# Cross attention and mixture of experts: query weights turned first, and the places of the attention's steps in the expert loop changed

## The reference

```python
x = x + xattn(layernorm(x), ctx, ctx, mask, Wq, bq, Wk, bk, Wv, bv)   # 154 keys per batch
x = x + ffn(layernorm(x), gate_w, w_gate, w_up, w_down, sw_gate, sw_up, sw_down)

# ffn: 16 experts of width 128, the best 8 by a normed gate, and one shared expert
logits = l2norm(xf) @ l2norm(gate_w).T
scores = sigmoid(logits); topk_scores, idx = top_k(scores, 8)      # weights: topk / their sum
y = einsum('neh,ehd->ned', silu(xf @ w_gate) * (xf @ w_up), w_down)
out = sum over experts of y * weight + silu(xf @ sw_gate) * (xf @ sw_up) @ sw_down
```

## Time and profile before

| | us |
|---|---|
| median of 3 runs | 645.16 (644.83 to 646.23) |
| the profiled execution | 644.59 |
| its span | 642.5 |

### The profile page before, as it was taken

How to read it: one execution, slowest core, us unless ns; L and a number is a source line. 1 busy time by engine, 2 the same in 40 slices (tenths; PEclk the granted TensorE clock), 3 DMA queues, 4 the chain that set the end, 5 groups by cost and what they waited for, 6 DMA issues and landing times.

```text
span 642.5 us, 10415 instructions
## 1 busy us (share of the span) xinstructions
PE 632.0 (98%) x3690; PEld 550.4 (86%) x3690; DVE 462.6 (72%) x925; ACT 235.8 (37%) x500; POOL 274.5 (43%) x261
## 2 busy tenths in 40 slices
PE   7999989999999999999999999999999999999997
PEld 7688878888888888889888888898888888888886
DVE  3788797758876688767877688775896668575444
ACT  5745444323243423333242333434234332423221
POOL 2517476343632346233553336433553334423442
PEclk9999999999999999999999999999999999999999
DMA  7456653523325314233334232253240431243100
GB/s 205 100 183 187 183 149 65 198 72 102 67 35 197 108 67 98 73 129 107 93 71 166 70 137 66 34 199 97 76 99 29 171 108 41 59 121 112 65 2 33
DMA packets 112513, 67.04 MB, mean 104 GB/s; under 512 B 80982, under 2 KB 102255, under 8 KB 112463
## 3 DMA queue, kind: packets, MB, share of 16 engines
q1 hardware_dynamic: 111374, 65.61, 35.6%
q10 hardware_dynamic: 1088, 0.79, 0.4%
HBM read 55.66 MB, written 10.42 MB: 103 GB/s over the span
## 4 chain that ended last, share of the span: by engine, by line
PE 88%; DVE 3%; DMA 2%; issue 2%; POOL 2%; ACT 1%; SPq 1%; POOLq 0%; ACTq 0%; DVEq 0%
PE y_ps L397 9%; PE gate_ps L399 9%; PE up_ps L399 9%; PE y_ps L398 9%; PE gate_ps L398 9%; PE up_ps L398 9%; PE y_ps L399 9%; PE up_ps L397 9%; PE gate_ps L397 9%; PE f_ps L545 2%; POOL hidden L1358 1%; DMA cb<-c_rows 1%; PE f_ps L582 1%; DVE hs L1168 1%; PE f_ps L584 1%
## 5 line engine op out<-in xcount | busy, mean ns | idle before, releaser
L1358 POOL TENSOR_TENSOR hidden<-hidden,cb 128x512 f32<-128x512 f32 x128 | 193.0, 1509 | 281.3 <-DVE hidden L1162 237.7
L880 ACT ACTIVATE hidden<-gate_ps 128x512 f32<-128x512 f32 x136 | 81.3, 598 | 282.5 <-PE gate_ps L399 282.4
L1158 DVE SCALAR_TENSOR_TENSOR hidden<-hidden,gate_ps 128x512 f32<-128x512 f32 x136 | 92.7, 682 | 98.4 <-ACT hidden L880 98.3
L397 PE MATMUL y_ps<-W,hs 128*128 128x256 f32 x544 | 154.3, 284 | 2.3 <-DVE hs L1168 2.3
L398 PE MATMUL y_ps<-W,hs 128*128 128x256 f32 x544 | 151.5, 278 | 0.0
L399 PE MATMUL y_ps<-W,hs 128*128 128x256 f32 x544 | 151.2, 278 | 0.0
L1168 DVE TENSOR_TENSOR hs<-hidden,hs 128x512 fp32r<-128x512 f32 x136 | 102.3, 752 | 25.5 <-ACT hs L887 25.0
L397 PEld LDWEIGHTS y_ps<-W,hs 128*128 128x128 f32 x544 | 102.2, 188 | 9.4 <-issue 3.6
L397 PE MATMUL gate_ps<-xT,W 128*128 128x512 f32 x272 | 107.3, 394 | 0.0
L399 PE MATMUL gate_ps<-xT,W 128*128 128x512 f32 x272 | 107.1, 394 | 0.0
L399 PE MATMUL up_ps<-xT,W 128*128 128x512 f32 x272 | 106.9, 393 | 0.0
(11 more groups left out here) (164 smaller groups left out, 641.9 us busy)
## 6 DMA issues: line engine op xcount, KB each, us to landing
cb<-c_rows SPq DMA_DIRECT2D x64, 512.0 KB, 4.7
blocks<-in_x_dram SPq DMA_DIRECT2D x28, 128.0 KB, 2.9
xin<-in_x_dram SPq DMA_DIRECT2D x7, 512.0 KB, 4.0
t_rows<-blocks SPq DMA_DIRECT2D x28, 128.0 KB, 2.7
xs<-t_rows SPq DMA_DIRECT2D x7, 512.0 KB, 3.5
out_dram<-x SPq DMA_DIRECT2D x7, 512.0 KB, 5.6
p_rows<-blocks SPq DMA_DIRECT2D x28, 80.0 KB, 2.3
stage<-in_L_ffn_w_gate_dram SPq DMA_DIRECT2D x16, 128.0 KB, 2.6
```

The lines of the kernel that those rows point to most:

```text
L397: mm(ps, lh, rh, start=first and i == 0, stop=False)
L880: af(ew[:, i, :], gate_ps[:, i, :], ACT.Tanh, scale=0.5).then_inc(tanh_done, 1)
L1158: V_.scalar_tensor_tensor(out=ew[:, i, :], in0=ew[:, i, :], scalar=1.0, in1=gate_ps[:, i, :], op0=ALU.add, op1=ALU.mult).then_inc(silu_don ...
L1358: pg.tensor_tensor(h[:, i, :], ew[:, i, :], cb[:, pair % PLACES, (e - 1) % 2, :], ALU.mult) \
```

## The change

In the loop the tables move by half a step: `swap_p` from the end to the middle of step 2, `probs_hi` and `probs_lo` from 5 to 4.5, `attend` from (5.5, 6) to (5, 5.5), `residual`, `ln2`, `ln2_scale` and `swap_x2` by half a step likewise, and `ln2_std` from (7.5, 7.5) to (6.5, 7.5). In the first loop's DMA order `store_probs(1)` and `load_probs(1)` move ahead of one `load_stage` each.

At the start, Wq is loaded and turned ahead of the context, with 17 idle turns ahead of it in place of 20 (`WARM`); `wqT` is written by VectorE and not by ScalarE; x's first half is loaded behind the context's tails and its second half ahead of the small tensors; the first scores stand ahead of `turn_ctx_rest`; ScalarE's order changes (the exponentials ahead of `read_ctx_rest`, `split_hi(1)` behind `write_vt_hi`); and `load_x_blocks(1)` stands ahead of `load_stage(4)`. `keys_by_wq_first` waits for `kt_read` itself, since `bias_row_first`, which did so, now stands behind it.

```diff
--- before.py
+++ after.py
@@ -19,18 +19,18 @@
 
 
 
-PE_AT = dict(scores=(0, .5), attend=(5.5, 6), logits=(12,), turn_z=(12.5,), turn_c=(14.5,))
-ACT_AT = dict(exps=(1.5, 2), probs_hi=(5,), t2_hi=(11.5,), read_z=(12.5,), tanh_scores=(13,), combine_rows=(15,))
-DVE_AT = dict(maxes=(.5, 1.5), swap_p=(2.5,), sum_reciprocal=(3.5,), probs_lo=(5,), residual=(6, 6.5),
-              ln2=(6.5, 7), ln2_scale=(8, 8.5), swap_x2=(8.5,), t2_lo=(11.5,), sum_logits=(13,), top_eight=(13.5,),
+PE_AT = dict(scores=(0, .5), attend=(5, 5.5), logits=(12,), turn_z=(12.5,), turn_c=(14.5,))
+ACT_AT = dict(exps=(1.5, 2), probs_hi=(4.5,), t2_hi=(11.5,), read_z=(12.5,), tanh_scores=(13,), combine_rows=(15,))
+DVE_AT = dict(maxes=(.5, 1.5), swap_p=(2,), sum_reciprocal=(3.5,), probs_lo=(4.5,), residual=(5.5, 6),
+              ln2=(6, 6.5), ln2_scale=(7.5, 8), swap_x2=(8,), t2_lo=(11.5,), sum_logits=(13,), top_eight=(13.5,),
               weights=(13.5,))
-POOL_AT = dict(ln2_std=(7.5, 7.5), inverse_norm=(8.5,))
+POOL_AT = dict(ln2_std=(6.5, 7.5), inverse_norm=(8.5,))
 
 DVE_SOON = dict(ln1=(10, 10.5), swap_x=(15.5,))
 POOL_SOON = dict(add_bias=(12.5,), ln1_std=(11.5, 11.5))
 
 POOL_FIRST = dict(ln1_std=(.5, .5))
-WARM = 20
+WARM = 17
 
 
 def xattn_moe_kernel(nc, x, ctx, mask, Wq, bq, Wk, bk, Wv, bv, gate_w, w_gate, w_up, w_down,
@@ -322,16 +322,16 @@
 
             sp.dma_start(ctx_main[:, 0, :], ctx[0, 0:P, :]).then_inc(ctx0_loaded, 16)
-            sp.dma_start(xin[:, 0:2, :], x_rows[0][:, 0:2, :]).then_inc(x_half, 16)
             sp.wait_ge(tail_zeroed, 1)
             for b in range(B):
                 sp.dma_start(ctx_tail[PAD * b:PAD * b + TAIL, :], ctx[b, P:KEYS, :]).then_inc(ctx0_loaded, 16)
+            sp.dma_start(xin[:, 0:2, :], x_rows[0][:, 0:2, :]).then_inc(x_half, 16)
+            sp.dma_start(xin[:, 2:4, :], x_rows[0][:, 2:4, :]).then_inc(x_loaded, 16)
             sp.dma_start(bk_col[:], bk.rearrange("(k p) -> p k", p=P), allow_slow_non_contiguous=True) \
                 .then_inc(bk_loaded, 16)
             sp.dma_start(bq_col[:], bq.rearrange("(k p) -> p k", p=P), allow_slow_non_contiguous=True) \
                 .then_inc(bq_loaded, 16)
             sp.dma_start(mask_in[:], mask.rearrange("(t p) k -> p t k", p=P)).then_inc(mask_loaded, 16)
-            sp.dma_start(xin[:, 2:4, :], x_rows[0][:, 2:4, :]).then_inc(x_loaded, 16)
             sp.dma_start(ctx_main[:, 1:B, :], ctx[1:B, 0:P, :].rearrange("b p d -> p b d")).then_inc(ctx1_loaded, 16)
             sp.dma_start(bv_row[:], bv.partition_broadcast(1)).then_inc(bv_loaded, 16)
             sp.dma_start(wv_in, Wv.rearrange("(k p) e -> p k e", p=P)).then_inc(wv_loaded, 16)
@@ -339,8 +339,8 @@
             for e in range(STAGES):
                 load_stage(e)
             load_stage(STAGES)
+            load_x_blocks(1)
             load_stage(STAGES + 1)
-            load_x_blocks(1)
             move_v_tails()
             load_x(1)
             load_stage(STAGES + 2)
@@ -353,10 +353,10 @@
             load_stage(EARLY + 3)
             spread(0, PLACES)
             load_stage(EARLY + 4)
+            store_probs(1)
             load_stage(EARLY + 5)
-            store_probs(1)
+            load_probs(1)
             load_stage(EARLY + 6)
-            load_probs(1)
             spread(0, PLACES + 1)
             for e in range(EARLY + 7, NE):
                 load_stage(e)
@@ -451,6 +451,7 @@
 
             def keys_by_wq_first():
                 pe.wait_ge(wqT_read, 1)
+                pe.wait_ge(kt_read, 2)
                 for k in range(KD):
                     for m in range(KD):
                         ins = mm(gate_ps[:, 1, k * KEYS:(k + 1) * KEYS], wqT[:, m, k * P:(k + 1) * P],
@@ -654,17 +655,17 @@
 
             pe.sem_inc(down_done, FREE)
             keep_warm()
+            turn_wq()
             turn_ctx_first()
             turn_x_first(0)
             keys_first()
-            turn_wq()
-            bias_row_first()
             turn_x_first(1)
             keys_by_wq_first()
+            bias_row_first()
+            scores(0, 0)
+            scores(0, 1)
             turn_ctx_rest(0)
             turn_ctx_rest(1)
-            scores(0, 0)
-            scores(0, 1)
             value_tails()
             values(0, y_ps[:, 0, 0:D])
             turn_p_first(0)
@@ -717,8 +718,8 @@
             af = nc.scalar.activation
 
             def load_weights():
+                act.dma_start(wq_in, Wq.rearrange("(k p) e -> p k e", p=P)).then_inc(wq_loaded, 16)
                 act.dma_start(wk_in, Wk.rearrange("(k p) e -> p k e", p=P)).then_inc(wk_loaded, 16)
-                act.dma_start(wq_in, Wq.rearrange("(k p) e -> p k e", p=P)).then_inc(wq_loaded, 16)
 
             def read_ctx_first():
                 act.wait_ge(ctx_turned, 1)
@@ -734,14 +735,6 @@
                 act.wait_ge(ctx_turned, 2 + k)
                 af(ctxT[:, k, 1:B, 0:P], (up_ps, gate_ps)[k][:, 0, 0:(B - 1) * P].rearrange("p (b c) -> p b c", c=P),
                    ACT.Copy).then_inc(ctxT_read, 1)
-
-            def write_wqT():
-
-                act.wait_ge(wq_turned, 1)
-                act.wait_ge(wq_mean, 1)
-                for m in range(KD):
-                    ins = af(wqT[:, m, :], gate_ps[:, 0, m * D:(m + 1) * D], ACT.Identity, bias=wq_sum[:, KD + m:KD + m + 1])
-                ins.then_inc(wqT_read, 1)
 
             def write_keep(t0, t1):
                 act.wait_ge(mask_loaded, 16)
@@ -907,24 +900,23 @@
             read_t1_first(0)
             read_keys_first()
             write_keep(0, 2)
-            write_wqT()
+            read_t1_first(1)
+            read_a_first()
+            bias_row_first()
             read_ctx_tails()
-            bias_row_first()
             router_norms()
-            read_a_first()
-            read_t1_first(1)
             write_keep(2, 4)
+            split_hi(0)
+            exps(0, 0)
+            exps(0, 1)
             read_ctx_rest(0)
             read_ctx_rest(1)
-            split_hi(0)
-            split_hi(1)
-            exps(0, 0)
-            exps(0, 1)
             vt_hi_first()
             write_v_hi(0, y_ps[:, 0, 0:D])
             probs_hi_first(0)
             probs_hi_first(1)
             write_vt_hi()
+            split_hi(1)
             read_keys_rest(0)
             read_keys_rest(1)
             split_hi(2)
@@ -985,6 +977,14 @@
                 dve.wait_ge(wq_summed, 1)
                 V_.tensor_scalar(wq_sum[:, KD:2 * KD], wq_sum[:, 0:KD], -1.0 / D, None, ALU.mult).then_inc(wq_mean, 1)
 
+            def write_wqT():
+
+                dve.wait_ge(wq_mean, 1)
+                for m in range(KD):
+                    ins = V_.tensor_scalar(wqT[:, m, :], gate_ps[:, 0, m * D:(m + 1) * D], wq_sum[:, KD + m:KD + m + 1],
+                                           None, ALU.add)
+                ins.then_inc(wqT_read, 1)
+
             def vt_lo_first():
                 dve.wait_ge(vt0_split, 1)
                 dve.wait_ge(v_hi, 1)
@@ -1214,13 +1214,14 @@
             for s_ in (silu_done, prod_done, h_lo):
                 dve.sem_inc(s_, FREE)
             dve.sem_inc(y_added, FREE)
+            mean_wq()
+            write_wqT()
             ln1(0, 0)
             spread_bq()
-            mean_wq()
             ln1(0, 1)
             add_bias_first(0)
+            mask_and_max(0, 0)
             add_bias_first(1)
-            mask_and_max(0, 0)
             mask_and_max(0, 1)
             vt_lo_first()
             write_v_lo(0, y_ps[:, 0, 0:D])
```

## The result

The changed kernel takes **658.41 us** (median of 6, 657.18 to 661.74) against 644.97 (644.20 to 646.23) for the kernel before on the same chip: ratio 1.021, 95% interval 1.0189 to 1.0232. I forecast 652.5 and a range up to 655.0: the sign is right, the size is not. The profiled execution took 658.88, its span is 657.0.

A forecast was written before the change was run, and what follows sets the result against it. TensorE, 98% busy, was taken as the bound. Steady waits of 8.0 less 0.3 (first loop) and 0.4 (start) gave +7.3 on the 642.5 span, 649.8; with 2.09 beyond the span and 0.57 to the median, 652.5 us, range 645.8 to 655.0.

The forecast's parts named there:

- what can be won and lost: TensorE: at most 3.2 us to win in the first loop, nothing in chunks 2 to 7, where moves can only harm.
- the steady step and its price: Steady loops, `down` 9: a new wait of 1.33 us (0.35 plus 0.98 for GpSimd's weighting delaying the second scaling), six times, 8.0.
- the bare 0.35: Steady loops: the wait at `down` 9 from second scaling and transposes ahead of expert 9's `hs`, without GpSimd; 2.1 us over six.
- Rival (a): Steady loops: the second scaling goes ahead of GpSimd's weighting, so the waits sum to 2.1 us, total 646.6; chance 14%.
- Cost: 0: Steady loops: the probabilities are ready at 146.1, `attend` at 5 wants them at 146.95; 0.8 us of room, no gain or loss.
- Rival (c): Steady loops: a GpSimd operation delays the subtractions, so attention waits 0.3 to 0.8 us more six times, 654 to 657; chance 8%.
- Tokens leave about 0.3 us sooner than today, the logits with them: First loop, logits' turn: turned tokens and logits come about 0.3 us sooner, giving the loop's gain of 0.3 us.
- the wait at `down` 9: First loop: the two waits of 2.1 us in sum become one of 2.1 to 2.8, with `hs` 9 at 86.9 to 87.5.
- SyncE's order as the cap: First loop: the tokens' move stands on SyncE behind `load_stage(16)`, which waits for `split_lo(13)`, now behind the transposes.
- TensorE's arrival at `down` 10: First loop: TensorE comes to `down` 10 at 91.2 to 91.8 us instead of 92.41.
- Gain 0.4 us: Start: the residual stands 0.9 us sooner, but a later stage 4 leaves 0.4; bounds 0.9 and -0.5.
- Stage 4's new wait: Start: `load_stage(4)` waits for `split_lo(1)`, issues at 24.3 to 25.7 instead of from 19.71, landing 3 us later at 28.3.

The follow-up runs named there:

- the turn back at 8.5: Changed kernel with the second half's `ln2_scale` and `swap_x2` put back from 8 to 8.5: 646.21 us, ratio 1.0008 to the kernel before.
- both scalings at 7.5: Changed kernel with the second half's `ln2_scale` moved from 8 to 7.5, `swap_x2` still at 8: 650.57 us, ratio 1.0062 to the kernel before.
- the added GpSimd operation: Changed kernel plus one small GpSimd operation ahead of expert 10's weighting in each chunk, so the weighting starts later: 652.73 us, ratio 1.0110 to the kernel before.
- the loop alone: Kernel before, with its own start, plus all the change's tables and its SyncE order in the loop: 657.66 us, ratio 1.0165 to the kernel before.
- the kept-busy kernel: Changed kernel plus 20 turns of the identity on TensorE ahead of `down` 9 in the first loop: 657.89 us, ratio 1.0213 to the kernel before.
- The later bias: Changed kernel with GpSimd's `add_bias` for the chunk after next at 13.5 instead of 12.5: 656.05 us, ratio 1.0162 to the kernel before.
- the bias first: Changed start with the older loop, and `add_bias_first(1)` moved ahead of `mask_and_max(0, 0)`: 646.38 us, ratio 1.0028 to the kernel before.
- the start alone: Changed kernel with the loop's tables and SyncE's probability order put back as before: 648.34 us, ratio 1.0009 to the kernel before.
- probabilities alone: Kernel before with only `swap_p` at 2, `probs_hi` and `probs_lo` at 4.5 and the change's SyncE order: 645.30 us, ratio 0.9999 to the kernel before.
- start and probabilities: Changed start with `add_bias_first(1)` ahead of `mask_and_max(0, 0)`, older loop, but probabilities half an expert sooner: 643.63 us, ratio 0.9970 to the kernel before.
- loop with the turn back: Kernel before, own start, plus the change's loop with second `ln2_scale` and `swap_x2` at 8.5: 647.32 us, ratio 1.0022 to the kernel before.

## Why the prediction was wrong in size

**Right: what can be won and lost.** TensorE has no slack, so each steady wait counts whole, and one wait a chunk is six. The marks go up by 1.38, 1.54, 1.45 and 1.44 in chunks 3 to 6 (the wait's 1.28, and the matmuls of `down` 9 take 0.1 more behind it).

**Right: the steady step and its price.** Forecast 1.33 each, 8.0 in all; measured 1.28 each, 7.7 in all. Each part of it has its own experiment: the turn back at 8.5 takes all of it away, and so do both scalings at 7.5; the added GpSimd operation leaves the bare 0.35 to 0.5 and gives 5.7 us back, where 6 x 0.98 = 5.9 was the collision's share. Rival (a) had the order of the two wrong: `inverse_norm` ended at 166.21, L1359 started at 166.26, between the starts of the first scaling (166.10) and the second (166.42). The margin was narrow: I had GpSimd free 0.2 ahead of the product, it was free 0.03 behind it, and asked 0.16 ahead of the second scaling. But it came out so in all six loops. By the rule of the Trainium skill that I weighed there ("SBUF — State Buffer", section "Who interferes with whom") the one that asks first has the ports for its whole instruction. The trace agrees: the second scaling took 1.39 us behind L1359, and 0.41 when L1359 came later. It does not agree for the small added operation, which also came ahead of the second scaling (245.43 to 246.54, the scaling at 245.59) and left it at 0.41.

**Wrong by 0.9: "Cost: 0" for the attention at 5.** It held in five of six loops. In chunk 2's loop the attention waited 0.9. I had read the 0.8 of room in chunk 1's loop alone and took it for all. Rival (c) had this wait, but six times and from GpSimd; it came once, from DMA. In chunk 2's loop the way by DRAM is slower: from the block turn to ScalarE's first copy it takes 10.4 us (216.44 to 226.85) and in chunk 3's 8.6 (294.36 to 302.96), since the four stores took 3.62 to issue against 2.62 and landed in 3.2 against 2.3. SyncE, chunk 2 and chunk 3:

```profile
217.94 3.62 SPq L264 DMA_DIRECT2D p_rows<-blocks  x4
...
295.86 2.62 SPq L264 DMA_DIRECT2D p_rows<-blocks  x4
```

Six of the eight profiles with the attention at 5 show this wait, 0.5 to 0.9 us; the loop alone and the kept-busy kernel do not. It was to be seen in the trace of before, by reading each chunk's stores and not one: there the load of chunk 2's loop is issued 5.30 us behind the first store, and 4.25 us in the loops of chunk 1, 3 and 4 (chunks 1 and 2, kernel before):

```profile
136.17 2.62 SPq L264 DMA_DIRECT2D p_rows<-blocks  x4
140.42 0.33 SPq L270 DMA_DIRECT2D xn<-p_rows  x1
...
212.11 3.10 SPq L264 DMA_DIRECT2D p_rows<-blocks  x4
217.41 0.33 SPq L270 DMA_DIRECT2D xn<-p_rows  x1
```

**Wrong by 4.6: "Tokens leave about 0.3 us sooner than today, the logits with them".** This is the step that failed most. Ahead of it, the wait at `down` 9 was nearly right (`hs` 9 is ready at 88.77 with the start's 1.0 in it; 86.9 to 87.5 was forecast), and so was SyncE's order as the cap, with `split_lo` 13 behind the transposes. TensorE's arrival at `down` 10 was not: 91.2 to 91.8 was forecast, and it is 94.73, with 1.0 of the start and 1.6 of the low clock in it, which had no term. From SyncE's order I took that the tokens leave a little sooner. They leave 1.25 later, or 0.24 if the start's 1.01 is taken off; with the older start (the loop alone) it is 1.14. "The logits with them" is the larger error. Behind the leaving tokens three terms were put at nothing: the four stores take 1.12 more to issue, straight behind stage 16 and x; the load is issued 0.74 later behind them; and the two low parts take 2.21 more beside GpSimd. 0.24 + 1.12 + 0.74 + 2.21 = 4.31, and the marks say 4.32. The later bias brings the low parts from 3.50 to 1.37, of which 1.33 is its own. The collision that I had priced with care in the steady loop I did not look for at L1068, though GpSimd's `add_bias` and weighting are issued right there. The low clock is not a term of this sum: TensorE starts on the last `down` ahead of the logits 2.24 later than before (102.98 against 100.74), with the clock's 1.6 in it, and then still waits 3.1 for the tokens.

**Wrong by 1.4: "Gain 0.4 us" for the start.** Stage 4's new wait came, with `t2_hi` behind it, but later than forecast: issued at 26.27 and not 24.3 to 25.7, with `split_hi(4)` at 29.78 and not 28.3, on a DMA. The step that failed is one that I left out of the sum: `add_bias_first(1)` between the two maxes falls beside GpSimd's split, 1.81 for 0.48, and everything behind the second maxes waits. With the bias first it is 1.5 us less, as much as the error: there, with the first scores at the same 12.50, stage 4 is issued at 24.80, `split_hi(4)` starts at 28.11, and the mark is -0.49 where -0.4 was forecast. Besides, the marks scatter with how soon the first loads land: the first scores start between 11.30 and 12.50 us in the nine profiles with this start, and the changed kernel's profile is at the late end. The marks of the seven with the old place of the bias are -0.14 to +1.01, middle +0.32.

The sum so corrected: 7.7 and 0.6 (the matmuls behind the wait) and 0.9, 4.3 and 1.0 are 14.5, against 14.29 between the two profiled executions. What stays open is why the load of the first loop's probabilities takes 3.0 to 5.2 us, why chunk 2's stores are slower, why the last stores land later in some executions, and why a wait of TensorE is followed by the low clock in some executions only.

## What to carry to other kernels

When a step is moved past another, price it at all its places, not in the typical loop: the first loop, with its other queues, and the loop whose DMA is slowest had 5.2 of the 14.5 us here. Write down for each moved VectorE operation which GpSimd operation will be running beside it, in both directions; starting the weighting 1.1 us later was worth 5.7 us, with work added. And a wait that is taken away ahead of another one may give nothing: with the probabilities sooner, the attention's wait went and the time stayed, as `down` 10 waited longer.

## What was not expected of the hardware

- GpSimd's operations on whole tiles stop VectorE's until they end, on operations of several kinds: scaling 0.41 to 1.39 us behind L1359, the bias 0.48 to 1.81 beside a split of 1.81, the low part of the tokens 0.69 to 1.72 and 1.86. GpSimd's small operation on 128x4 (1.11 us) beside the scaling cost it nothing (0.73 for the pair), nor did the weighting beside the transposes (2.09).
- The load of the probabilities in the first loop, from issue to ScalarE's first copy with ScalarE waiting for it: 3.0 us before and in the changed kernel, 4.4 with the start alone, 5.2 with the bias first, at issue times within 0.9 us of each other (before, start alone, bias first). With the weighting later it is 4.8, issued at 62.58, where the changed kernel has 3.0, issued at 62.84 in the same order.
- The last two stores of 256 KB took 2.1 us from issue to landing before and in the changed kernel, and 3.3 with the start and the probabilities (medians of the two); the span ends 1.8 us later by it.
- Behind waits of TensorE of 2.4 to 2.6 us at `down` 9 or 10 (by the step), the clock was granted at 0.50 for 3.4 us in four profiles (the changed kernel, turn back, probabilities alone, start and probabilities) and stayed at 1.00 in three (loop alone, loop with the turn back, bias later). Behind 3.15 us (both scalings at 7.5) it was 6.8 us. Behind the attention's wait in the first loop, of 2.5 to 3.3 us (start alone, weighting later, start with the bias first), it came each time. Behind the logits' wait of 2.6 to 3.3 us (the changed kernel, loop alone, kept busy, weighting later) it never came. The length of the wait alone does not decide it.
